# Edge stage of a graph network: GpSimd takes 768 columns of one multiplication and the remaining denominators' sums

## What is computed

```
H = x @ weight.T
C = alpha_src[None, :] + alpha_dst[:, None]
Tau = adj.T * exp(max(0.2 * C, C))
Z = (adj.T * Tau / sum(Tau, axis=1, keepdims=True)) @ H
x = layernorm(x + Z)
```

## Time and profile before

| | |
|---|---|
| median of 3 executions | 11376.24 us (11374.95 to 11376.49) |
| profiled execution, its own time | 11372.95 us |
| span of the profiled execution | 11371.2 us |
| PE busy | 10347.5 us, 91% of the span |
| DVE busy | 9970.1 us, 88% |
| ACT busy | 10362.4 us, 91% |
| POOL busy | 8141.1 us, 72% |
| mean granted clock of TensorE | 0.974 of full speed |

### The profile page before, as it was taken

The page is one execution under the profiler, slowest core; times in us unless marked ns, Lnnn a source line. Parts: engine busy times, 40 slices in busy tenths (PEclk is TensorE's granted clock), DMA queues, the critical chain, the costliest instruction groups (busy, mean ns, idle before and its releaser), DMA issues. The chain is left out here.

```text
span 11371.2 us, 371147 instructions
## 1 busy us (share of the span) xinstructions
PE 10347.5 (91%) x138582; PEld 5321.7 (47%) x138582; DVE 9970.1 (88%) x10702; ACT 10362.4 (91%) x8620; POOL 8141.1 (72%) x4114
## 2 busy tenths in 40 slices
PE   5749999999999999999799999999999999999988
PEld 4614555555545555555344444444444444444474
DVE  7348999999989999999799999999899999999958
ACT  3149999999999999999899999999999999999925
POOL 0007888888878888888688888888788888888800
PEclk7979999999999999999899999999999999999999
DMA  8694443433454433433433333333433333333364
GB/s 331 217 254 77 62 62 61 62 61 62 62 94 62 62 61 61 62 61 62 90 54 53 55 55 55 54 54 55 93 54 54 55 55 54 53 55 55 52 197 178
DMA packets 505827, 943.45 MB, mean 83 GB/s; under 512 B 100743, under 2 KB 453390, under 8 KB 454702
## 3 DMA queue, kind: packets, MB, share of 16 engines
q1 hardware_dynamic: 505740, 942.28, 42.4%
HBM read 799.88 MB, written 142.00 MB: 83 GB/s over the span
## 5 line engine op out<-in xcount | busy, mean ns | idle before, releaser
L1101 DVE SCALAR_TENSOR_TENSOR a_probs<-ps,a_adj 128x768 f32<-128x768 f32 (+1 forms) x9216 | 8976.8, 1020 | 776.3 <-PE ps L991 663.4
L1076 POOL TENSOR_TENSOR a_pool_probs<-a_pool_probs,a_adj 128x768 f32<-128x768 f32 (+1 forms) x4096 | 8124.6, 1984 | 1860.7 <-ACT a_pool_probs L1051 1860.7
L1056 ACT ACTIVATE a_probs<-a_probs 128x1536 f32<-128x1536 f32 (+3 forms) x4096 | 8207.4, 2004 | 12.6 <-DVE a_probs L1101 12.2
L991 PE MATMUL ps<-a_q,a_k 34*128 34x384 f32 (+1 forms) x26624 | 4457.4, 406 | 650.6 <-ACT a_pool_probs L1051 367.7
L1051 ACT ACTIVATE a_pool_probs<-ps 128x768 f32<-128x768 f32 (+1 forms) x4096 | 4486.9, 1095 | 32.6 <-PE ps L991 32.5
L1011 PE MATMUL ps<-a_probs,a_v 128*9 128x192 f32 (+1 forms) x73728 | 4012.9, 341 | 0.0
L991 PEld LDWEIGHTS ps<-a_q,a_k 34*128 34x128 f32 x26624 | 2180.5, 185 | 3179.4 <-ACT a_pool_probs L1051 1187.8
L1011 PEld LDWEIGHTS ps<-a_probs,a_v 128*9 128x9 f32 x73728 | 1952.1, 91 | 1273.0 <-issue 126.4
L1011 PE MATMUL ps<-a_pool_probs,a_v 128*9 128x192 f32 (+1 forms) x32768 | 2218.9, 343 | 2.3 <-POOL a_pool_probs L1076 2.2
L1011 PEld LDWEIGHTS ps<-a_pool_probs,a_v 128*9 128x9 f32 x32768 | 489.5, 89 | 986.3 <-issue 980.6
L571 POOL MEMSET v_rows<- 128x512 f32 x2 | 1.9, 1054 | 480.1 <-POOLq L83 480.1
(11 more groups left out here) (177 smaller groups left out, 2104.7 us busy)
## 6 DMA issues: line engine op xcount, KB each, us to landing
a_k<-k_parts SPq DMA_DIRECT2D x2048, 208.0 KB
a_v<-v_ext SPq DMA_DIRECT2D x512, 117.0 KB, 3.4
adj_t<-tr SPq DMA_DIRECT2D x26, 1664.0 KB, 6.4
g0tile<-adj_t SPq DMA_DIRECT2D x26, 1664.0 KB, 6.9
g2tile<-adj_t SPq DMA_DIRECT2D x26, 1664.0 KB, 7.0
nat<-in_adj SPq DMA_DIRECT2D x25, 1663.5 KB, 10.1
e_nat<-in_adj SPq DMA_DIRECT2D x25, 1663.5 KB, 6.8
a_q<-q_parts SPq DMA_DIRECT2D x2048, 12.0 KB
```

The costliest lines, as they stand in the source:

```text
L991: ins = nc.tensor.matmul(ps[:, place + bank:place + bank + half], k_tile[b][row:row + SCORE_ROWS, P * j:P * (j + 1)].bitcast(F32R), q_tile ...
L1056: nc.scalar.activation(sums, sums, ACT.Exp, scale=2.0).then_inc(sums_exped, 1)
L1076: nc.gpsimd.tensor_tensor(flat(k), flat(k), adj_c[:, j, :], ALU.mult).then_inc(multiplied, 1)
L1101: v.scalar_tensor_tensor(out=halves(flat(k)), in0=score(j), scalar=SCALE / 2, in1=halves(adj_c[:, j, :]), op0=ALU.mult, op1=ALU.add).then_ ...
```

## The change

GpSimd multiplies the last 768 columns of `e_both` (columns 2560 to 3327) in place of VectorE, and adds the last 256 columns of `e_tau` to `e_den_of`. VectorE keeps `e_tau` and the first 2560 columns of `e_both`. A semaphore `share_ready` tells of GpSimd's part. TensorE waits for it at the bank that starts at column 2560, and SP before it loads over `e_nat`. VectorE waits for `rest_added` of the block two before, since GpSimd's add reads `e_tau`.

```diff
+EDGE_SPLIT = 5 * BANK
...
         def _(sp):
             for i in range(EDGE_LOADS, BLOCKS):
                 sp.wait_ge(both_ready, i - EDGE_LOADS + 1)
+                sp.wait_ge(share_ready, i - EDGE_LOADS + 1)
                 edge.load(sp, adj, i)
...
                 pe.wait_ge(both_ready, i + 1)
                 for at in range(0, NP, BANK):
                     to = min(at + BANK, NP)
+                    if at == EDGE_SPLIT:
+                        pe.wait_ge(share_ready, i + 1)
                     ins = nc.tensor.matmul(ps[:, at:to], h[0:rows, i, :], both[i % 2][0:rows, at:to],
                                            start=begin and to < NP, stop=end, skip_group_check=True)
...
             nc.gpsimd.memset(ones[:, :], 1.0).then_inc(padded, 1)
+            pool.wait_ge(padded, EDGE_LOADS + 2)
+            for i in range(BLOCKS):
+                b, rows = i % 2, rows_of[i]
+                pool.wait_ge(tau_ready, i + 1)
+                if i >= 2:
+                    pool.wait_ge(weighed, i - 1)
+                nc.gpsimd.tensor_tensor(both[b][0:rows, EDGE_SPLIT:NP], tau[b][0:rows, EDGE_SPLIT:NP],
+                                        nat[i % EDGE_LOADS][0:rows, EDGE_SPLIT:NP], ALU.mult).then_inc(share_ready, 1)
+                if i >= 1:
+                    pool.wait_ge(rest_added, i)
+                nc.gpsimd.tensor_tensor(den_of[0:rows, :], den_of[0:rows, :], tau[b][0:rows, 4 * DEN_COLS:NP], ALU.add
+                                        ).then_inc(rest_added, 1)
...
                 if i >= 2:
                     dve.wait_ge(summed, i - 1)
+                    dve.wait_ge(rest_added, i - 1)
                 v.tensor_tensor(tau[b][0:rows, :], edges[b][0:rows, :], nat_i[0:rows, :], ALU.mult).then_inc(tau_ready, 1)
                 dve.wait_ge(tau_ready, i + 1)
                 if i >= 2:
                     dve.wait_ge(weighed, i - 1)
-                v.tensor_tensor(both[b][0:rows, :], tau[b][0:rows, :], nat_i[0:rows, :], ALU.mult).then_inc(both_ready, 1)
-                if i >= 1:
-                    dve.wait_ge(rest_added, i)
-                v.tensor_tensor(den_of[0:rows, :], den_of[0:rows, :], tau[b][0:rows, 4 * DEN_COLS:NP], ALU.add
-                                ).then_inc(rest_added, 1)
+                v.tensor_tensor(both[b][0:rows, 0:EDGE_SPLIT], tau[b][0:rows, 0:EDGE_SPLIT], nat_i[0:rows, 0:EDGE_SPLIT],
+                                ALU.mult).then_inc(both_ready, 1)
```

More of the change, by code:

```diff
@@ L1452, in edge_phase @@
         padded, chain, src_ready = mem.sem("e_padded"), mem.sem("e_chain"), mem.sem("e_src_ready")
-        cut, exped, tau_ready, both_ready, rest_added = (mem.sem("e_" + s) for s in (
-            "cut", "exped", "tau_ready", "both_ready", "rest_added"))
+        cut, exped, tau_ready, both_ready, share_ready, rest_added = (mem.sem("e_" + s) for s in (
+            "cut", "exped", "tau_ready", "both_ready", "share_ready", "rest_added"))
         summed, weighed = mem.sem("e_summed"), mem.sem("e_weighed")
```

## The result

The changed kernel takes 11398.45 us (median of 19 runs, 11391.39 to 11404.57). The kernel before, measured beside it, takes 11378.27 us (19 runs, 11373.68 to 11388.94). The ratio is 1.0017, with a 95% interval of 1.001 to 1.0024: 20 us slower, with 11 to 27 us inside the interval. The prediction took 0.2% (22.7 us) for what this kernel's measurement can tell from no change. The difference lies under that, yet the interval leaves out 1.

The account below looks back on a forecast made before the run. VectorE was taken to bound the edge stage at 7.53 us a block. With no overlap, 25 x (8.99 - 7.53) - 0.80 = +35.7 us on the 11376.2 us median gives 11412 us; range 11366 to 11426.

Parts of the forecast that it names:

- rival B: Edge stage: GpSimd's fixed part, perhaps half its column time too, overlaps VectorE; 11402 to 11374 us, middle 11388; chance 0.10.
- Rival A: Edge stage: free overlap, TensorE's 7.28 us the period if GpSimd costs VectorE under 1.14 us a block; 11369 us; chance 0.20.
- VectorE's own work, 6.39 us a block: Edge-stage block: VectorE's remaining work after losing 768 columns (0.80 us) and one add (0.34 us): 3.65 + 2.74 us.
- GpSimd's durations, 1.85 and 0.75 us: Edge-stage block: GpSimd's multiplication of 768 columns and add of 256, from attention-stage rows; together 2.60 us a block.
- "No overlap", 8.99 us: Edge-stage period if GpSimd's work never lies beside VectorE's: 6.39 + 2.60 us; the end the forecast took.
- The hand-overs, bounded at 21 us above: Between engines, outside the sum: GpSimd's at most 0.84 us a block, 21 us in 25 blocks; half taken as bound.
- New waits: Edge stage: TensorE's and SP's waits for GpSimd's share, VectorE's for its add; all covered by slack, costing nothing.
- "One path for both": GpSimd's reads of SBUF: 2.148 ns a column for two streams, twice VectorE's time, looks like one path for both.
- TensorE's floor: Edge-stage block: TensorE needs 7.53 - 0.25 = 7.28 us, the floor for anything that relieves VectorE alone.
- The clock at nothing: TensorE, idle 1.7 us of each edge-stage block, keeps granted clock 1.00 as in an earlier stage; costed at nothing.
- The 0.62 on the full sum: Chance given to the forecast itself: edge-stage loop slower by 35.7 us, 11412 us, own range 11402 to 11426.

## Why the prediction was right, and where its sum was off

Its direction held, and so did its mechanism in the main: GpSimd's reads and VectorE's two-input instructions exclude each other. Its size was nearly double: +35.7 us predicted, +20.2 measured, +21.7 in the loop. By the prediction's own signs a period of 7.5 to 8.6 us is rival B, partial overlap, and 8.43 us lies there. The result is inside the whole range because B and A had been taken into it, not because the forecast's sum was good.

- **VectorE's own work, 6.39 us a block: right.** With the holds taken off, e_tau is 3.62 us and e_both 2.82 in all runs.
- **GpSimd's durations, 1.85 and 0.75 us: right.** The run with one VectorE input has them at 1.85 and 0.73.
- **"No overlap", 8.99 us: the mis-sized term.** The engines do exclude each other, but only over GpSimd's columns. The hold is 1.62 us of 1.85 and 0.53 of 0.75. That is 0.45 us a block that the sum charged and VectorE didn't pay. Rival B named just this for its upper end (the fixed part alone, 8.60 us, 11402) and was given 0.10. It was nearest to the result. B's other half, that some of the time per column overlaps too, didn't happen.
- **VectorE's turn-around was left out.** Of the add's 0.53 us, 0.12 fall where VectorE waits for its own e_tau. With both corrections: 8.99 - 0.45 - 0.12 = 8.42 us against 8.43 measured.
- **The hand-overs, bounded at 21 us above: none were seen.** The shares' holds, drawn back to no columns, leave nothing over.
- **New waits cost nothing: right.** TensorE waits 1.17 us a block for e_both, and no computing engine waits for the share or the add. GpSimd's share ends 1.7 us after e_both does, inside the 4.5 us of cover. Only SP waits for the share before it issues its loads, and e_tau never waits for a load.
- **"One path for both" of GpSimd's two streams: not borne out.** The prediction read GpSimd's 2.148 ns a column as two streams through one path. One stream then should have cost half of 2.13, and the copy's hold was 0.81.
- **TensorE's floor was 7.20 us, not 7.28.** With GpSimd's reads gone it runs through with 0.0 idle. Rival A's figure would have been 11367 in place of 11369. Its condition was never met: GpSimd costs VectorE 2.03 us a block, above the 1.14 that decide.
- **The clock at nothing: right, on a weak ground.** The row that it rested on was followed, in the same trace, by 632 to 640 us with TensorE busy in 1.77 us and a granted clock of 0.61. In the changed kernel's loop the granted clock is 1.00, with 121.00 us busy of 140:

```profile
11160.00:11300.00 140.00, 121.00 (x491) 50.11 (x492) 139.45 (x34) 101.75 (x34) 140.00 (x34) 1.00 0.56 199
```

- **The chances.** Slower by more than 0.2% had 0.68, and the median landed at 0.17 to 0.18%, on the side that had 0.30. The 0.62 on the full sum was too sure: the trace had GpSimd's fixed 0.20 us in it, and I had put that to one side as a rival with nothing in the rows against it.

## What to carry to other kernels

Before giving GpSimd a piece of VectorE's work, count the SBUF inputs of the VectorE instructions that will run beside it. With two of them, GpSimd's time per column is taken from VectorE: 2.13 ns when GpSimd reads two inputs. VectorE's own time for a column is 1.04 ns, so where VectorE is the bound, moving such an operation loses at any size. GpSimd's copy, with one input, held it for 0.81 ns a column, less than 1.04; whether moving a one-input operation pays was not tested. Where VectorE reads one SBUF input (the other in PSUM, or a reduction), or where GpSimd only writes, GpSimd's work cost VectorE nothing here. Do the arithmetic with the slope of GpSimd's duration and not with the whole of it, and look at where VectorE waits for itself, since 0.11 us of a hold, or of a small instruction, disappears when it falls there.

## What the runs showed of the hardware that was not expected

- A blocked instruction isn't shown as idle time. It is written as busy and longer: GpSimd is busy in all of 140.00 us of the loop for 2.60 us of work in every 8.43.
- The exclusion covers only GpSimd's time per column. Its fixed 0.20 us overlap VectorE's work, in the add (0.53 us held of 0.73) and in shares of three sizes (0.53, 1.62 and 2.70 us held).
- The instruction that starts first isn't held. e_both, 0.04 us ahead of GpSimd's, keeps its 3.62 us with the add behind it and its 2.83 us with the share behind it.
- GpSimd's copy holds VectorE up by 0.81 ns a column and its two-input operation by 2.13, a ratio of 2.6 where the number of inputs says 2.
- Two VectorE instructions in sequence cost 0.11 us more when the second waits for the first's semaphore than when it doesn't (3.65 against 3.54 us), and moving the add, which the block has anyway, between them brought the block from 7.53 to 7.40 us.
